# Moving six pieces of work between slots and engine queues in the first layer of a two-layer cross-attention and feed-forward kernel

## The chip, the cores and the metric

One NeuronCore of a Trainium2 chip runs the whole kernel. The metric is the device time of one execution in microseconds (us); lower is better. The engines are TensorE (PE; its weight loads are listed as PEld), VectorE (DVE), ScalarE (ACT), GpSimd (POOL) and SyncE (SP), which only issues DMAs here. Each engine runs its own instruction queue in order; semaphores join them.

## The reference, cut to what matters

```python
# x: (32, 256, 256), ctx: (32, 77, 192); 16 heads of 64
x = x + xattn0(layernorm(x), ctx, Wq0, Wk0, Wv0, Wo0, bo0)
x = x + ffn0(layernorm(x), w_gate, w_up, w_down)      # hidden 768, weights are integers / 127
x = x + xattn1(layernorm(x), ctx, Wq1, Wk1, Wv1, Wo1, bo1)
x = x + ffn1(layernorm(x), rhs)                       # rows and rhs rounded to 8-bit steps, product, rescaled

def xattn(x, c, Wq, Wk, Wv, Wo, bo):
    q, k, v = heads(x @ Wq), heads(c @ Wk), heads(c @ Wv)
    return softmax(q @ k.T / 8, axis=-1) @ v @ Wo + bo
def ffn0(x, w_gate, w_up, w_down):
    h = silu(x @ wg.T) * (x @ wu.T)
    return h @ wd.T
def layernorm(x): return (x - mean(x)) / sqrt(var(x) + 1e-5)
```

## The kernel before, in words

A first part (to about 230 us) prepares the weights and makes the keys and values of all 32 batches. The second part is a software pipeline over 64 bodies, one for each batch of layer 0 and then of layer 1, plus two to drain; the first layer's bodies are numbered h = 0 to 31. A body has four slots, u = 0 to 3, one for each unit of four heads. Float32 operands are split into a float16 "high" part (a cast on ACT, `high`, L348) and a "low" remainder (a subtraction on DVE, `low`, L362), so products come in two or three terms.

In slot u of body h each engine takes these steps, in an order that is written out by hand:

- PE: `scores` of unit u (L1237), `queries` two units ahead, the output product `project` four units back, `weigh_values` three units back (L1274), and pieces of the feed-forward of older batches: `gate_up(c)` is the product of hidden block c (six of them, gate and up), `down` the product back. `gate_up(0)` and `gate_up(1)` of batch h-2 are in slot 3, 2 to 5 in the next body's slots 0 and 1, both `down` in slot 2. Their input x2T comes by a DMA transposition of x216, the split second normalised rows.
- ACT: casts of attention output (oT_h) and queries (qT_h), `exponentials(k, i, t)` in two halves t (L1426, four heads each), `tanh_gate(c)` (L1406), casts of hidden blocks (hT_h), and `normalise` (L352), which applies scale and shift to rows: x_pair (xn) from x_in for the layer's next input, yn from y.
- DVE: row maxima nmax (L1549), reciprocals rden (L1554), low parts, `sigmoid_gate` (sg, L1514) and `hidden` (hf, L1525), row spreads (L378), their `moments` (L384, then ve at L386), `normalise_rows` (x2, L373), `out_rows` (y, L1536), and x1 (L1692) at the end of slot 3.
- POOL: `probabilities` in two halves (pr L1712, cast L1725, low part L1717), low parts of four hidden blocks (hT_l, L1703), and for each of the three normalisations `inverse` (rs, a power, L395); for the first and third also `shift` (nmr, L399 and L402).
- SP: all loads, stores and DMA transpositions in one queue, in the order of the code: pT (probabilities, two for each unit), x2T (`turn_second_rows`, slot 2), xT (`turn_rows`), keys, values, rows.

The next input batch b = h+2 of layer 0 goes through: spreads and moments (DVE, slot 2), inverse and shift (POOL, slot 2), `normalise` to xn (ACT, last thing in slot 2), `cast_rows` (ACT, x16 high), `low_rows` (DVE, x16 low), `turn_rows` (SP: in slot 3 for the first three bodies, in slot 0 of the next body from body 4 on). x16 is read by `turn_rows` only. The two lines below show how the queues are tied around the first two of these steps:

```python
pool.wait_ge(s_var[k], count)   # inverse: waits for ve of moments
act.wait_ge(s_nmr[0], h + 2)    # before normalise(act, xn, x_in, rs1, 0, s_xn)
```

Of the kernel before, what the change touches and what calls it, by code (L numbers as in the profile page):

```python
# [51 lines left out]
def xattn_ffn_kernel(nc, x, ctx, wq0, wk0, wv0, wo0, bo0, w_gate, w_up, w_down,  # L52
# [29 lines left out]
    with stack:  # L82
# [33 lines left out]
        mv1 = sb("mv1", [P, QT, 2], F32)  # L116
        ve1 = sb("ve1", [P, QT], F32)
# [881 lines left out]
        def as_f16(bank):  # L999

            return bank[:, 0, :].bitcast(F16).rearrange("p (k q) -> p k q", q=NQ)
# [101 lines left out]
        with nc.Block() as block:  # L1103
# [117 lines left out]
            def _(pe):  # L1221
# [100 lines left out]
                def body(h, like, lay, plan, odd):  # L1322
# [9 lines left out]
                    for u in range(UNITS):  # L1332
# [7 lines left out]
                        if u == 3 and lay[-2] == 0:  # L1340
                            pe.wait_ge(s_x2d, 16 * (h - 1))
                            if like == 2:
                                pe.wait_ge(s_kvf, RING + LATE_BASE + LATE - 1)
                            gate_up(0, bank("gu", 0))
# [19 lines left out]
                        if u == 3 and lay[-2] == 0:  # L1364
                            if like == 2:
                                pe.wait_ge(s_kvf, RING + LATE_BASE + LATE)
                            gate_up(1, bank("gu", 1))
# [9 lines left out]
                        if u == 2 and lay[-2] == 1:  # L1377
                            pe.wait_ge(s_qi, h - 1 - B)
                            turn(pe, as_f16(bank("turned_q", 0)), q_i).then_inc(s_qt, 1)
                        if three is not None and (like, u) != (NB, 2):  # L1380
                            weigh_values(n + u - 3, (u - 3) % UNITS, 16 * (h + (u - 3) // UNITS + 1),
                                         32 * (h + (u - 3) // UNITS + 1), OV)
# [11 lines left out]
            def _(act):  # L1394
                def body(h, like, lay, plan, odd):
# [34 lines left out]
                    for u in range(UNITS):  # L1430
# [4 lines left out]
                        if u == 3 and lay[2] == 0:  # L1435
                            cast_rows(act, h + 2)
# [47 lines left out]
                        if u == 3 and lay[-2] == 0:  # L1484
                            tanh_gate(0, h - 2)
                        if u == 3 and lay[-3] == 0:
                            act.wait_ge(s_nmr[2], h - 2)
                            act.wait_ge(s_ys, 16 * (h - 2))
                            normalise(act, yn, y, rs3, 2, s_yn)
                        if u == 3 and lay[-2] == 0:  # L1490
                            tanh_gate(1, h - 2)
                        if lay[0] is not None:
                            exponentials(n + u, u % 2, 1)
# [11 lines left out]
            def _(dve):  # L1505
                def body(h, like, lay, plan, odd):
# [49 lines left out]
                    for u in range(UNITS):  # L1556
                        if u == 3 and lay[-3] == 0:
                            moments(dve, 2, st3, mv3, ve3, s_st3, s_mv3, h - 3)
                        if u == 3 and lay[2] == 0:
                            low_rows(dve, h + 2)  # L1560
# [24 lines left out]
                        if u == 2 and lay[-2] == 0:  # L1585
                            dve.wait_ge(s_x216h, h - 1)
                            low(dve, x216[:, :, 1, :], x2[:, :, :], x216[:, :, 0, :]).then_inc(s_x216l, 1)
# [11 lines left out]
                        if u == 2 and lay[2] == 0:  # L1599
                            moments(dve, 0, st1, mv1, ve1, s_st, s_mv, h + 2)  # L1600
                        if u == 2 and lay[0] is not None and lay[-2] == 0:
                            reciprocals(n + u, u % 2, 0)
# [80 lines left out]
                        if u == 3 and lay[-1] is not None:  # L1683
# [6 lines left out]
                            if lay[-2] == 1:  # L1690
                                dve.wait_ge(s_ysum, h - 1 - B)
                            dve.scalar_tensor_tensor(out=x1[odd][:, :, :], in0=OA, scalar=O_DOWN, in1=x_res[:, :, :],  # L1692
                                                     op0=ALU.mult, op1=ALU.add).then_inc(s_x1, 1)

# [4 lines left out]
            def _(pool):  # L1699
                def body(h, like, lay, plan, odd):  # L1700
# [27 lines left out]
                    for u in range(UNITS):  # L1728
                        if u == 0 and lay[-3] == 0:
                            low_hidden(0, h - 3)  # L1730
                        if u == 1 and lay[-3] == 0:
                            low_hidden(3, h - 3)
                        if (like, u) == (NB - 1, 3):
# [13 lines left out]
                        if u == 2 and lay[2] == 0:  # L1747
                            inverse(pool, 0, ve1, rs1, h + 2)
                            shift(pool, 0, mv1, rs1, h + 2)
# [40 lines left out]
```

## Time and profile before

| | |
|---|---|
| median of three runs | 1650.83 us (1649.32 to 1656.25) |
| profiled execution, its own time | 1644.11 us |
| span from the first to the last instruction | 1642.1 us |
| granted TensorE clock, mean | 0.995 |
| busy over the span: PE, PEld | 93%, 81% |
| busy over the span: DVE, ACT, POOL | 85%, 80%, 75% |

The busy shares are means over three unlike stages: the preparation, the first layer (about 270 to 1060 us) and the second layer (from about 1090 us). A matmul counts as busy for longer than it holds the array back, since matmuls overlap. What a change in the first layer is worth is to be read from that stage alone: from the distance between the same instruction in two neighbouring bodies, and from who waits for whom inside a body.

### The profile page before, as it was taken

Reading aid. Unit: us, or ns where it says so; the run is one execution under the profiler, and the core shown is the slowest. Engines: PE = TensorE matmul, PEld = TensorE weight load, DVE = VectorE, ACT = ScalarE, POOL = GpSimd, SP = SyncE. Lnnn points to the kernel's source line nnn. Section 1 sums busy time; section 2 is a strip of 40 time slices with the busy share of each in tenths; the row PEclk is TensorE's granted clock in tenths of the full one; section 3 lists DMA queues with packets and bytes.
Section 4 is the critical chain, followed back from the end, with each engine's and each line's share of the span. In section 5 each row is a group of like instructions: output and inputs, shape, how many; then the busy total and the mean of one; then the engine's idle time right before and its main releaser. Section 6 shows DMA issues by size and latency. Waiting matters only on the chain.

```text
span 1642.1 us, 75141 instructions
## 1 busy us (share of the span) xinstructions
PE 1523.7 (93%) x27410; PEld 1326.2 (81%) x27410; DVE 1402.9 (85%) x3522; ACT 1311.8 (80%) x5514; POOL 1239.0 (75%) x1966
## 2 busy tenths in 40 slices
PE   7999888999999999999999999999999999999995
PEld 4555568888888888888888888988888888888884
DVE  7777558988888898888988887899999999999996
ACT  6656678887878778788887877788888888888883
POOL 5110277778888788878878887879999999999984
PEclk9999999999999999999999999999999999999998
DMA  8998699877787777777777898889889898898995
GB/s 267 349 307 278 190 182 188 151 173 159 161 169 167 175 159 165 170 159 171 163 175 154 164 170 160 165 161 198 197 193 195 197 195 191 195 201 191 189 186 118
DMA packets 740023, 307.79 MB, mean 187 GB/s; under 512 B 629201, under 2 KB 725361, under 8 KB 737841
## 3 DMA queue, kind: packets, MB, share of 16 engines
q1 hardware_dynamic: 738049, 299.32, 83.2%
q0 software_dynamic: 1840, 6.82, 1.4%
q8 instruction: 68, 1.11, 0.3%
q14 instruction: 66, 0.54, 0.1%
HBM read 87.09 MB, written 65.54 MB: 93 GB/s over the span
## 4 chain that ended last, share of the span: by engine, by line
PE 26%; POOL 19%; DVE 15%; issue 15%; ACT 8%; DMA 3%; SPq 2%; DVEq 1%; ACTq 0%; POOLq 0%
PE psum L333 17%; POOL pr L1712 7%; POOL p L1725 5%; POOL p L1717 5%; PE psum L1237 4%; PE psum L1274 4%; ACT ex L1426 4%; DVE nmax L1549 3%; DVE x L373 2%; DVE oT_l L362 2%; DMA x2T<-x 2%; ACT yn L352 1%; POOL rs L395 1%; DVE sg L1514 1%; DMA pT<-p 1%
## 5 line engine op out<-in xcount | busy, mean ns | idle before, releaser
L1426 ACT ACTIVATE ex<-psum,nmax 128x77 f32<-128x77 f32 x2048 | 636.1, 335 | 40.5 <-DVE nmax L1549 31.1
L1712 POOL TENSOR_TENSOR pr<-ex,rden 128x308 f32<-128x308 f32 x512 | 385.9, 754 | 81.7 <-DVE rden L1554 77.7
L1426 ACT ACTIVATION_READ_ACCUMULATOR ex<-psum,nmax 128x1 f32 x2048 | 443.4, 217 | 0.0
L1717 POOL TENSOR_TENSOR p<-pr,p 128x308 f16<-128x308 f32 x512 | 388.9, 760 | 40.7
L333 PE MATMUL psum<-xT,wq_h 128*64 128x256 f16 x4064 | 353.9, 276 | 0.8 <-DMA xT<-x 0.8
L1549 DVE TENSOR_REDUCE nmax<-psum 128x4 f32<-128x308 f32 x512 | 237.4, 464 | 57.4 <-PE psum L1237 57.2
L333 PE MATMUL psum<-xT,wq_l 128*64 128x256 f16 x2032 | 280.9, 273 | 0.0
L333 PE MATMUL psum<-wo_h,oT_h 128*64 128x256 f16 x1792 | 250.5, 276 | 27.7 <-DVE oT_l L362 27.4
L1725 POOL CAST p<-pr 128x308 f16<-128x308 f32 x509 | 238.8, 469 | 38.4 <-DMA pT<-p 5.8
L333 PE MATMUL psum<-wo_l,oT_h 128*64 128x256 f16 x1792 | 249.0, 274 | 0.0
L333 PE MATMUL psum<-wo_h,oT_l 128*64 128x256 f16 x1792 | 248.9, 274 | 0.0
L333 PEld LDWEIGHTS psum<-xT,wq_h 128*64 128x64 f16 x4064 | 208.4, 110 | 14.9 <-DMA xT<-x 0.9
L1274 PE MATMUL psum<-pT,vb 77*64 77x256 f16 x3072 | 212.8, 274 | 5.3 <-DMA pT<-p 5.3
L348 ACT ACTIVATE oT_h<-psum 128x512 f16<-128x512 f32 x256 | 153.5, 600 | 69.3 <-PE psum L1274 64.2
L1237 PEld LDWEIGHTS psum<-kb,qT_h 64*128 64x128 f16 x4096 | 115.1, 94 | 96.0 <-issue 96.0
L1237 PE MATMUL psum<-kb,qT_h 64*128 64x77 f16 x4096 | 145.1, 197 | 38.5 <-ACT ex L1426 19.7
L1274 PEld LDWEIGHTS psum<-pT,vb 77*64 77x64 f16 x3072 | 164.6, 110 | 15.6 <-issue 12.5
L362 DVE TENSOR_TENSOR oT_l<-psum,oT_h 128x512 f16<-128x512 f32 x256 | 174.2, 680 | 2.3 <-ACT oT_h L348 2.2
L365 DVE SCALAR_TENSOR_TENSOR qT_l<-psum,qT_h 128x512 f16<-128x512 f32 x256 | 173.1, 676 | 0.0
L348 ACT ACTIVATE qT_h<-psum 128x512 f16<-128x512 f32 x256 | 153.1, 598 | 3.5 <-PEq L412 3.5
L333 PEld LDWEIGHTS psum<-wo_h,oT_h 128*64 128x64 f16 x1792 | 102.3, 110 | 45.9 <-DVE oT_l L362 40.8
L1237 PE MATMUL psum<-kb,qT_l 64*128 64x77 f16 x2048 | 134.7, 194 | 0.0
(173 smaller groups left out, 3425.6 us busy)
## 6 DMA issues: line engine op xcount, KB each, us to landing
keys<-ks SPq DMA_DIRECT2D x16, 1232.0 KB, 7.4
kb<-keys SPq DMA_DIRECT2D x256, 77.0 KB, 2.7
vb<-vals SPq DMA_DIRECT2D x128, 154.0 KB
vals<-vs SPq DMA_DIRECT2D x64, 256.0 KB, 4.3
x_pair<-in_x_dram SPq DMA_DIRECT2D x32, 256.0 KB
pT<-p SPq DMA_TRANSPOSE x512, 3.3
x_res<-in_x_dram SPq DMA_DIRECT2D x32, 256.0 KB, 3.1
mid_x<-y SPq DMA_DIRECT2D x32, 256.0 KB, 2.5
```

The source lines that it names most:

```text
L333: last = pe.matmul(o[b * DH:(b + 1) * DH], w[:, b * DH:(b + 1) * DH], x, **flags)
L348: return act.activation(dst, src, ACT.Copy, scale=scale)
L362: return dve.tensor_tensor(dst, src, hi, ALU.subtract)
L365: return dve.scalar_tensor_tensor(out=qT_l[i][:, :, :], in0=src, scalar=Q_DOWN, in1=qT_h[i][:, :, :], op0=ALU.mult, op1=ALU.subtract)
L373: dve.tensor_scalar(dst[:, t, :], src[:, t, :], mv[:, t, 0:1], rs[:, t:t + 1], ALU.subtract, ALU.mult).then_inc(s_done, 1)
L1237: last = pe.matmul(SC[:, b, at], w[rows, a, t * P:(t + 1) * P], kb[u // 2][rows, b, part, u % 2 * PPU + a, :], start=(q == 0), stop=(q == ...
L1274: last = pe.matmul(o[b * DH:(b + 1) * DH, a, :].rearrange("p (t q) -> p t q", q=P), vb[u // 2][:, part, c:c + DH], pT[u][0:NK, b, at:at + ...
L1426: last = act.activation(ex[i][:, t, b, :], SC[:, t, b * NK:(b + 1) * NK], ACT.Exp, bias=nmax[i][:, t, b:b + 1], accum_out=den[i][:, t, b:b ...
L1549: dve.tensor_reduce(nmax[i][:, t, :], SC[:, t, :].rearrange("p (h k) -> p h k", k=NK), AX_X, ALU.max, negate=True).then_inc(s_m, 1)
L1712: pool.tensor_tensor(pr[:, t, :, :], ex[i][:, t, :, :], r, ALU.mult).then_inc(s_p, 1)
L1717: pool.tensor_tensor(d[:, t, 1, :, 0:NK], pr[:, t, :, :], d[:, t, 0, :, 0:NK], ALU.subtract).then_inc(s_pl, 1)
L1725: pool.tensor_copy(p16[v % 2][:, t, 0, :, 0:NK], pr[:, t, :, :]).then_inc(s_ph, 1)
```

## The change

Six moves, all in bodies that handle layer 0; no instruction is added, removed or resized.

1. PE, slot 3: `gate_up(0)` goes from behind `scores` to behind `queries`; `gate_up(1)` from behind `queries` to behind `project`.
2. ACT, slot 3: `cast_rows` goes from the head of the slot to behind `tanh_gate(0)`.
3. ACT, slot 3: `tanh_gate(1)` goes from ahead of the second half of the exponentials to behind it.
4. DVE, slot 3: `low_rows` goes from the head of the slot to its very end, behind x1.
5. DVE, slot 2: the low part of x216 goes from ahead of the spreads and moments of the next rows to behind them.
6. POOL, slot 2: `inverse` and `shift` of the next rows go from behind `probabilities(u-1, half 1)` to ahead of it.

```diff
--- before.py
+++ after.py
@@ -1337,11 +1337,6 @@
                             gate_up(4, bank("gu", 4))
                         if lay[0] is not None:
                             scores(n + u, u, 32 * (h + 1))
-                        if u == 3 and lay[-2] == 0:
-                            pe.wait_ge(s_x2d, 16 * (h - 1))
-                            if like == 2:
-                                pe.wait_ge(s_kvf, RING + LATE_BASE + LATE - 1)
-                            gate_up(0, bank("gu", 0))
                         if ("q", u) in plan:
                             if u == 2 and lay[1] == 0:
                                 pe.wait_ge(s_xd, 16 * (h + 1))
@@ -1362,9 +1357,10 @@
                             pe.wait_ge(s_nl, 16 * (h + 2 - B))
                             turn(pe, bank("turned_x", 0), xn).then_inc(s_xt, 1)
                         if u == 3 and lay[-2] == 0:
+                            pe.wait_ge(s_x2d, 16 * (h - 1))
                             if like == 2:
-                                pe.wait_ge(s_kvf, RING + LATE_BASE + LATE)
-                            gate_up(1, bank("gu", 1))
+                                pe.wait_ge(s_kvf, RING + LATE_BASE + LATE - 1)
+                            gate_up(0, bank("gu", 0))
                         if (like, u) == (NB, 2):
                             weigh_values(n + u - 3, (u - 3) % UNITS, 16 * (h + (u - 3) // UNITS + 1),
                                          32 * (h + (u - 3) // UNITS + 1), OV_END)
@@ -1377,6 +1373,10 @@
                         if u == 2 and lay[-2] == 1:
                             pe.wait_ge(s_qi, h - 1 - B)
                             turn(pe, as_f16(bank("turned_q", 0)), q_i).then_inc(s_qt, 1)
+                        if u == 3 and lay[-2] == 0:
+                            if like == 2:
+                                pe.wait_ge(s_kvf, RING + LATE_BASE + LATE)
+                            gate_up(1, bank("gu", 1))
                         if three is not None and (like, u) != (NB, 2):
                             weigh_values(n + u - 3, (u - 3) % UNITS, 16 * (h + (u - 3) // UNITS + 1),
                                          32 * (h + (u - 3) // UNITS + 1), OV)
@@ -1432,8 +1432,6 @@
                             high_hidden(0, h - 3)
                         if u == 1 and lay[-3] == 0:
                             high_hidden(2, h - 3)
-                        if u == 3 and lay[2] == 0:
-                            cast_rows(act, h + 2)
                         if lay[-1] is not None:
                             act.wait_ge(s_pv, n + u - 3)
                             high(act, oT_h[u % 2][:, :, :], weighed(like, u)).then_inc(s_oh, 1)
@@ -1483,14 +1481,16 @@
                                  bank("turned_x", 0).rearrange("p k (t q) -> p t k q", q=P)).then_inc(s_xh, 1)
                         if u == 3 and lay[-2] == 0:
                             tanh_gate(0, h - 2)
+                        if u == 3 and lay[2] == 0:
+                            cast_rows(act, h + 2)
                         if u == 3 and lay[-3] == 0:
                             act.wait_ge(s_nmr[2], h - 2)
                             act.wait_ge(s_ys, 16 * (h - 2))
                             normalise(act, yn, y, rs3, 2, s_yn)
+                        if lay[0] is not None:
+                            exponentials(n + u, u % 2, 1)
                         if u == 3 and lay[-2] == 0:
                             tanh_gate(1, h - 2)
-                        if lay[0] is not None:
-                            exponentials(n + u, u % 2, 1)
                         if u == 2 and lay[2] == 0:
                             act.wait_ge(s_nmr[0], h + 2)
                             act.wait_ge(s_x16l, h + 1)
@@ -1556,8 +1556,6 @@
                     for u in range(UNITS):
                         if u == 3 and lay[-3] == 0:
                             moments(dve, 2, st3, mv3, ve3, s_st3, s_mv3, h - 3)
-                        if u == 3 and lay[2] == 0:
-                            low_rows(dve, h + 2)
                         if lay[(u - 1) // UNITS] is not None:
                             reciprocals(n + u - 1, (u - 1) % 2, 1)
                         if lay[0] is not None:
@@ -1582,9 +1580,6 @@
                         if u == 1 and lay[-3] == 0:
                             sigmoid_gate(4, h - 3)
                             hidden(4, h - 3)
-                        if u == 2 and lay[-2] == 0:
-                            dve.wait_ge(s_x216h, h - 1)
-                            low(dve, x216[:, :, 1, :], x2[:, :, :], x216[:, :, 0, :]).then_inc(s_x216l, 1)
                         if u == 1 and lay[-2] == 1 and like <= NB:
                             normalise_rows(dve, 1, x2, x1[1 - odd], mv2, rs2, h - 1, s_x2)
                         if late_tile(like, u) is not None:
@@ -1598,6 +1593,9 @@
                             spreads(dve, x_in, st1, s_st)
                         if u == 2 and lay[2] == 0:
                             moments(dve, 0, st1, mv1, ve1, s_st, s_mv, h + 2)
+                        if u == 2 and lay[-2] == 0:
+                            dve.wait_ge(s_x216h, h - 1)
+                            low(dve, x216[:, :, 1, :], x2[:, :, :], x216[:, :, 0, :]).then_inc(s_x216l, 1)
                         if u == 2 and lay[0] is not None and lay[-2] == 0:
                             reciprocals(n + u, u % 2, 0)
                         if lay[(u + 1) // UNITS] is not None:
@@ -1691,6 +1689,8 @@
                                 dve.wait_ge(s_ysum, h - 1 - B)
                             dve.scalar_tensor_tensor(out=x1[odd][:, :, :], in0=OA, scalar=O_DOWN, in1=x_res[:, :, :],
                                                      op0=ALU.mult, op1=ALU.add).then_inc(s_x1, 1)
+                        if u == 3 and lay[2] == 0:
+                            low_rows(dve, h + 2)
 
                 bodies(dve, body)
 
@@ -1730,6 +1730,9 @@
                             low_hidden(0, h - 3)
                         if u == 1 and lay[-3] == 0:
                             low_hidden(3, h - 3)
+                        if u == 2 and lay[2] == 0:
+                            inverse(pool, 0, ve1, rs1, h + 2)
+                            shift(pool, 0, mv1, rs1, h + 2)
                         if (like, u) == (NB - 1, 3):
                             weights_of(h, 2, 1)
                         elif (like, u) == (NB, 0):
@@ -1744,9 +1747,6 @@
                             low_hidden(2, h - 3)
                         if u == 0 and (lay[-2] == 0 or lay[-3] == 0):
                             inverse(pool, 1, ve2, rs2, h - 1)
-                        if u == 2 and lay[2] == 0:
-                            inverse(pool, 0, ve1, rs1, h + 2)
-                            shift(pool, 0, mv1, rs1, h + 2)
                         if (like, u) == (NB - 1, 3):
                             weights_of(h, 3, 0)
                             low_of(h, 2, 1)
```

## Rows read from the trace of the kernel before

**Rows 1.** Waits over the span: us in total, times, longest.
```profile
ACT x_pair L352 <- POOL nmr L402: 88.8, 30, 3.1
```

**Rows 2.** Chain that ended last, 685 to 740 us: start, us, what.
```profile
719.15 0.20 POOL nmr L402
...
726.75 0.63 PE psum L1237 x24
```

**Rows 3.** Timeline, DVE's normalise_rows, one a body: start, us, instruction.
```profile
292.94 1.76 DVE L373 TENSOR_SCALAR x<-x,mv,rs 128x256 f32<-128x256 f32 x2
...
734.58 1.77 DVE L373 TENSOR_SCALAR x<-x,mv,rs 128x256 f32<-128x256 f32 x2
760.82 1.26 DVE L373 TENSOR_SCALAR x<-x,mv,rs 128x256 f32<-128x256 f32 x2
...
891.05 1.77 DVE L373 TENSOR_SCALAR x<-x,mv,rs 128x256 f32<-128x256 f32 x2
```

**Rows 4.** Timeline of DVE in one body, slots 2 and 3.
```profile
714.20 0.83 DVE L362 TENSOR_TENSOR x<-x 128x512 f16<-128x512 f32 x1
...
716.13 0.72 DVE L386 TENSOR_SCALAR ve<-mv 128x2 f32<-128x2 f32 x1
...
719.47 0.56 DVE L386 TENSOR_SCALAR ve<-mv 128x2 f32<-128x2 f32 x1
721.33 0.71 DVE L362 TENSOR_TENSOR x<-x_pair,x 128x512 f16<-128x512 f32 x1 [1.30 <-ACT x L348]
...
725.41 0.42 DVE L1514 SCALAR_TENSOR_TENSOR sg<-th,psum 128x256 f32<-128x256 f32 x1 [0.37 <-ACT th L1406]
...
727.37 0.48 DVE L1549 TENSOR_REDUCE nmax<-psum 128x4 f32<-128x308 f32 x1 [0.24 <-PE psum L1237]
```

**Rows 5.** Timeline of POOL in the same body.
```profile
714.54 0.79 POOL L1725 CAST p<-pr 128x308 f16<-128x308 f32 x1
...
716.12 0.70 POOL L1712 TENSOR_TENSOR pr<-ex,rden 128x308 f32<-128x308 f32 x1
716.89 0.44 POOL L1725 CAST p<-pr 128x308 f16<-128x308 f32 x1
...
718.12 0.69 POOL L395 TENSOR_TENSOR rs<-ve,half_neg 128x2 f32<-128x2 f32 x1
...
719.30 0.70 POOL L1712 TENSOR_TENSOR pr<-ex,rden 128x308 f32<-128x308 f32 x1
...
721.30 0.72 POOL L395 TENSOR_TENSOR rs<-ve,half_neg 128x2 f32<-128x2 f32 x1
...
726.55 0.70 POOL L1712 TENSOR_TENSOR pr<-ex,rden 128x308 f32<-128x308 f32 x1 [1.99 <-DVE rden L1554]
...
731.70 0.67 POOL L1703 TENSOR_TENSOR hT_l<-hf,hT_h 128x256 f16<-128x256 f32 x1 [0.42 <-ACT hT_h L348]
```

**Rows 6.** Timeline of ACT in the same body, slot 3.
```profile
724.00 1.11 ACT L352 ACTIVATE yn<-y,nmr,rs 128x256 f32<-128x256 f32 x2
724.99 0.40 ACT L1406 ACTIVATE th<-psum 128x256 f32<-128x256 f32 x1
```

**Rows 7.** A pair two hundred us on: DVE's low_rows, then POOL's power.
```profile
929.60 0.72 DVE L362 TENSOR_TENSOR x<-x_pair,x 128x512 f16<-128x512 f32 x1 [1.14 <-ACT x L348]
...
929.73 1.17 POOL L395 TENSOR_TENSOR rs<-ve,half_neg 128x2 f32<-128x2 f32 x1
```

**Rows 8.** SP and PE around x2T, and its landing time over the span.
```profile
715.54 1.26 SPq L1133 DMA_TRANSPOSE x2T<-x  x1
...
719.05 0.63 PE L333 MATMUL psum<-x2T,wgT 128*64 128x256 f16 x8
...
721.26 0.60 PE L333 MATMUL psum<-x2T,wgT 128*64 128x256 f16 x8
...
1006.58 0.63 PE L333 MATMUL psum<-x2T,wgT 128*64 128x256 f16 x8 [0.74 <-DMA x2T<-x]
...
DMA to landing us min/median/max: 3.3/3.4/5.2
```

## The prediction

> **What bounds the kernel now.** I read the waits over the whole span first. The largest one with an end to it on the first layer is ACT's: it stands about 3 us in each of 30 bodies before it can normalise the next rows, because POOL's shift comes late [rows 1]. A wait of an engine is worth nothing until it is on the chain, so the chain was read next, over two bodies around 712 us. It runs through POOL's probabilities to the shift at 719.15, then ACT's normalise and cast, DVE's low_rows, the exponentials of unit 3 and the scores of the next body at 726.75 [rows 2]. So the wait is on the path. The third view is one instruction that comes once a body. From 292.94 to 891.05 there are 24 of them, 23 periods, 26.00 us each [rows 3]; the period after a 1.77 us one is 26.24 us. 13 of the 24 take 1.77, the others 1.26; the short ones save 0.51 of the period. Last, the timelines of one body: DVE there idles only 1.30 us before low_rows, 0.37 before the second sg, 0.24 before the first maximum of the next body [rows 4]. That is 1.9 us in 26.24. DVE is the second bound, close behind the chain: of the 3 us that ACT waits, no more than about 1.9 can come back, and only if these three idles all vanish.
>
> **The moves, one by one**, in the times of the body of rows 4 to 6. No instruction is added, so each term is a start that moves.
>
> *DVE slot 2, POOL slot 2.* The x216 low part (0.83; the next instruction follows 0.75 later) leaves the place ahead of the spreads, so ve of the next rows comes to issue at 716.13 - 0.75 = 715.38 [rows 4]. POOL's cast beside that low part took 0.79 where the next cast took 0.44; without it POOL is free 0.35 earlier, at 716.12 - 0.35 = 715.8 [rows 5]. Power and shift can start at 715.9 instead of 718.12. But the low part now stands in DVE's queue straight behind ve, and the power waits for that same ve. What that does is seen at 929.6: low_rows began 0.13 before the power, and the power took 1.17 instead of 0.72 [rows 5, 7]. I take this 0.45, since the order of issue in the new code is the order of that pair; the lower bound is 0, from the power at 718.12. Then rs ends at 717.1 and nmr at 717.1 + (719.35 - 718.81) = 717.6, where 719.35 is the end of the shift and 718.81 that of the power [rows 2, 5]. ACT's normalise starts 1.7 us earlier. POOL's probabilities of the held half start at 717.1 + 0.5 = 717.6 instead of 716.12, last 2.0 (716.12 to 718.12), and the next half, at 719.30 before, starts at 719.6; its successor, the third norm's power, goes from 721.30 to 721.6. So nmr for yn is there at about 722.8 instead of 722.6.
>
> The Trainium skill (SBUF — State Buffer, section "Who interferes with whom") says that a DVE instruction with two SBUF inputs and a GpSimd instruction that reads SBUF hold the shared pair as an exclusive lock, and that the order of issue decides who blocks. The pair at 929.6 agrees (1.17 against 0.72). By that rule the low part behind ve stops the power for its whole length, and by the row for 0.45; either way the sum below stays within its bounds.
>
> *x2T.* The low part ends about 1.7 us later (about 716.75), so SP issues x2T at 716.8 instead of 715.54, and at 3.4 us to landing it is there at 720.2 [rows 8]. gate_up(0), at 719.05 before, stands behind the queries now. gate_up(0) and the queries, 40 matmuls, took 719.05 to 721.26, so the 24 of the queries take 1.33 and it comes at 720.4. The delay is covered by some 0.2 us. If the cover is gone, tanh_gate(0) comes late; it has about 0.4 until yn. SP's two pT issues behind x2T slip by 1.3 too; their reader, weigh_values in slot 0 of the next body, is far behind. I cost this at 0.
>
> *DVE slot 3, the head.* low_rows is gone, and with it the wait of 1.30. ve of the third norm cannot start sooner than about 719.4, since the second half of y waits for PE's second down product, and PE is dense. It ends, with POOL's instruction of that time, near 719.7, and the first maximum follows at 719.8; before it followed low_rows (721.33) by 0.7, at 722.0. It comes 2.2 us earlier, and the exponentials of unit 3, behind its 0.5, at 720.3.
>
> *ACT slot 3.* One half of the exponentials takes 1.2 (from the tanh at 724.99 to the scores at 726.75, less 0.3 for the tanh's step and 0.25 for the hand-over). So: exponentials 1.2, tanh_gate(0) 0.3, cast_rows 0.5 (0.63 less the overlap): ACT is free at 722.3, and yn waits for nmr until 722.8 (before: 724.00 [rows 6]). yn takes 1.0 (724.00 to 724.99), the second half of the exponentials 1.2, so tanh_gate(1), now behind them, starts at 725.0. It started at 724.99. Everything that was won ahead of it is spent: the exponentials end 1.4 us sooner, the tanh does not move.
>
> *DVE slot 3, the tail.* sg, hf, a reciprocal and x1 follow that tanh as before: sg at 725.45 against 725.41. Then comes low_rows. sg to the first maximum took 727.37 - 0.24 - 725.41 = 1.72 without its wait, 0.15 of it a last reciprocal, so low_rows issues 1.6 after sg, at 727.0, while POOL's pr of unit 3, which starts 0.24 after the reciprocal (726.55 before), holds on till 727.25 [rows 5]; low_rows without a hold needs 0.55 (0.83 less the 0.28 that pr covered at 714.20). It is done at 727.8, and the first maximum of the next body comes at 727.8 instead of 727.37: **+0.43 us**. Before, this maximum waited for the scores; they are now ready 1.3 us ahead, which is worth nothing. DVE is dense from there to slot 3, so the delay is passed on.
>
> *Given back.* PE's gate_up(3) is ready earlier, so ACT's tanh and the cast of hidden block 2 come 0.2 sooner against DVE, and POOL's low part of it, which waited 0.42 for that cast [rows 5], too. DVE's ve of the second norm ends with this POOL instruction, as ve at 716.13 ended with pr (716.85 and 716.82). **-0.2 us**; bounds 0 and -0.45, about the hold of rows 7.
>
> **The sum.** 0.43 - 0.2 = +0.23 us in each of the 27 bodies that have every step (h = 3 to 29): +6. In the four bodies behind them (from 976 us) there are no next rows, x2T lands late and PE stands 0.74 for it [rows 8]; the queries now fill that: 4 x -0.74 = -3. In the first three bodies turn_rows stands on SP in slot 3 behind low_rows, 5 us later than before, with the loads of x_res and keys queued behind it; these are needed late in the next body: 0 to +1, I take 0. Total +3 on the profiled 1644.1 us. The median of the runs shown is 6.7 us above that execution (1650.83 to 1644.11), so 1650.8 + 3 = **1654 us**.
>
> **The rivals.** I call "no change" what lies within 0.5% (8.3 us), about what a measurement of this kernel can tell.
>
> *Faster: the power is not held.* If it gets the port ahead of the low part (or reads its few values at once), nmr for yn is there at 722.35, ACT is the limit, and all of slot 3 shifts by 0.45: 27 x (0.23 - 0.45) - 3 = -9, about 1642. It gains another 0.24 a body (-6, 1636) if normalise_rows always takes 1.26: a mean 0.51 x 13/24 is lost now. For it: the power at 721.30 took only 0.72 with low_rows starting 0.03 behind it [rows 4, 5]. Against: there the power was first. Chance 0.27.
>
> *Slower: the tail is not given back.* If ve of the second norm stays held by POOL, for POOL's prob chain is itself held by low_rows (its cast waits until 727.8) and the low part of block 2 starts no earlier, the +0.43 stands, and up to 0.55 with a full collision: 27 x 0.5 - 3 = +10, 1661. It decides at the POOL instruction that runs when ve issues near 731.8. Chance 0.22.
>
> *Slower: POOL wins at normalise_rows.* It takes 1.77 or 1.26, in one body or the next, with nothing else changed [rows 3]: I read this as a race for the port with POOL's next instruction. If the new phase loses it in all bodies, 27 x 0.51 x 11/24 = +6 on top: 1660. Chance 0.09.
>
> *Nothing moves the end*, as worked out: 0.42, its own range 1648 to 1659.
>
> **Numbers.** 1654 is the likeliest case. The range 1638 to 1668 reaches from well into the first rival to both slower ones together. Faster by over 0.5% 0.27, within 0.42, slower 0.31.
>
> **What would show it.** In the trace after, in a steady body: the wait of ACT for nmr of the next rows falls from 3.1 to about 1.2; the power of the next rows takes about 1.17 and stands ahead of the first probabilities of slot 2; DVE waits some 2 us before its second sg (0.37 before) and none before the first maximum; low_rows takes about 0.8; the period, from normalise_rows, is 26.0 to 26.5. If the wait before sg is under 1 us, or the period is under 25.7, tanh_gate(1) comes earlier than I say and the prediction is wrong on the fast side. If PE waits for x2T, the cover was too thin and it is wrong on the slow side.

## The result and the profile after

The changed kernel takes 1657.26 us, the median of 20 runs (1653.88 to 1666.07), against 1649.16 us for the kernel before, also 20 runs on the same chips (1644.9 to 1656.25). The ratio is 1.0049 [1.0036, 1.0063]: slower by 0.5%, by more than the scatter of the runs and just inside what I called no change (8.1 us of 8.3). Forecast were 1654 us and a range of 1638 to 1668.

The profiled execution spans 1655.9 us against 1642.1. Of these 13.8 us, 5.4 lie ahead of the first normalise_rows of all (246.94 against 241.59). In the preparation of the weights POOL's one wait for DVE's moments (ve L608 <- mv L803) is 62.3 against 56.4, and the change doesn't touch that part. I put the 5.4 down to the execution: the twelve kernels below, which hold the same edits or parts of them, have 55.6 to 59.1 there. The times of the two profiled executions fit this: the one before is some 5 below its median, the one after 0.8 above. The rest, 8.4, is about that of the medians (8.1), and is told here.

Waits of the kernel after over the span (us, times, longest), beside [rows 1]:

```profile
ACT ex L1426 <- DVE nmax L1549: 93.9, 120, 1.6
DVE sg L1514 <- ACT th L1406: 85.9, 53, 2.8
...
ACT x_pair L352 <- POOL nmr L402: 38.8, 30, 1.6
```

The same view of the kernel before has these two:

```profile
ACT ex L1426 <- DVE nmax L1549: 31.1, 96, 1.1
...
DVE sg L1514 <- ACT th L1406: 12.2, 31, 1.1
```

ACT's wait for the mean product of the next rows fell from 88.8 to 38.8, what the change sets out to do. But DVE now waits 74 us longer for the tanh, and ACT 63 longer for the maxima. Fifty microseconds of waiting went, and more came back elsewhere.

DVE in one steady body, slots 2 and 3, and the normalise_rows on both sides (answers to [rows 3, 4]):

```profile
718.36 1.77 DVE L373 TENSOR_SCALAR x<-x,mv,rs 128x256 f32<-128x256 f32 x2
...
725.40 0.47 DVE L386 TENSOR_SCALAR ve<-mv 128x2 f32<-128x2 f32 x1
725.78 0.68 DVE L362 TENSOR_TENSOR x<-x 128x512 f16<-128x512 f32 x1
...
729.66 0.45 DVE L1549 TENSOR_REDUCE nmax<-psum 128x4 f32<-128x308 f32 x1
...
735.44 0.42 DVE L1514 SCALAR_TENSOR_TENSOR sg<-th,psum 128x256 f32<-128x256 f32 x1 [2.72 <-ACT th L1406]
...
736.99 0.83 DVE L362 TENSOR_TENSOR x<-x_pair,x 128x512 f16<-128x512 f32 x1
...
737.83 0.44 DVE L1549 TENSOR_REDUCE nmax<-psum 128x4 f32<-128x308 f32 x1
...
744.82 1.26 DVE L373 TENSOR_SCALAR x<-x,mv,rs 128x256 f32<-128x256 f32 x2
```

POOL in that body (answers to [rows 5]):

```profile
725.95 1.06 POOL L395 TENSOR_TENSOR rs<-ve,half_neg 128x2 f32<-128x2 f32 x1
...
727.36 0.20 POOL L402 TENSOR_TENSOR nmr<-nmr,rs 128x2 f32<-128x2 f32 x1
...
736.58 0.70 POOL L1712 TENSOR_TENSOR pr<-ex,rden 128x308 f32<-128x308 f32 x1 [1.79 <-DVE rden L1554]
...
741.93 0.67 POOL L1703 TENSOR_TENSOR hT_l<-hf,hT_h 128x256 f16<-128x256 f32 x1 [0.26 <-ACT hT_h L348]
```

ACT in slots 2 and 3 (answers to [rows 6]):

```profile
727.67 1.09 ACT L352 ACTIVATE x_pair<-x_pair,nmr,rs 128x256 f32<-128x256 f32 x2 [1.28 <-POOL nmr L402]
...
732.82 1.09 ACT L352 ACTIVATE yn<-y,nmr,rs 128x256 f32<-128x256 f32 x2 [0.49 <-POOL nmr L402]
...
735.02 0.38 ACT L1406 ACTIVATE th<-psum 128x256 f32<-128x256 f32 x1
```

Three distances divide the body. From normalise_rows to the second tanh: 735.02 - 718.36 = 16.66, and before 26.24 - (734.58 - 724.99) = 16.65. From that tanh to the first maximum of the next body: 737.83 - 735.02 = 2.81 against 727.37 - 724.99 = 2.38, so +0.43. From there to normalise_rows: 744.82 - 737.83 = 6.99 against 734.58 - 727.37 = 7.21, so -0.22 [rows 3, 4, 6]. The rows came earlier, the tanh did not, and low_rows behind it costs what it costs.

Normalise_rows over the first layer:

```profile
298.74 1.76 DVE L373 TENSOR_SCALAR x<-x,mv,rs 128x256 f32<-128x256 f32 x2
...
902.09 1.77 DVE L373 TENSOR_SCALAR x<-x,mv,rs 128x256 f32<-128x256 f32 x2
...
1005.42 1.67 DVE L373 TENSOR_SCALAR x<-x,mv,rs 128x256 f32<-128x256 f32 x2
...
1023.81 0.42 DVE L1514 SCALAR_TENSOR_TENSOR sg<-th,psum 128x256 f32<-128x256 f32 x1 [1.60 <-ACT th L1406]
...
1032.44 1.67 DVE L373 TENSOR_SCALAR x<-x,mv,rs 128x256 f32<-128x256 f32 x2
...
1109.24 1.65 DVE L373 TENSOR_SCALAR x<-x,mv,rs 128x256 f32<-128x256 f32 x2
```

and of the kernel before, the lines of the last bodies that its rows ahead do not have:

```profile
993.82 1.07 DVE L373 TENSOR_SCALAR x<-x,mv,rs 128x256 f32<-128x256 f32 x2
...
1010.38 0.42 DVE L1514 SCALAR_TENSOR_TENSOR sg<-th,psum 128x256 f32<-128x256 f32 x1 [0.36 <-ACT th L1406]
...
1013.23 0.48 DVE L1549 TENSOR_REDUCE nmax<-psum 128x4 f32<-128x308 f32 x1 [1.23 <-PE psum L1237]
...
1020.29 1.07 DVE L373 TENSOR_SCALAR x<-x,mv,rs 128x256 f32<-128x256 f32 x2
...
1095.13 1.64 DVE L373 TENSOR_SCALAR x<-x,mv,rs 128x256 f32<-128x256 f32 x2
```

The 23 steady periods take 603.35 / 23 = 26.23 us against 26.00 [rows 3]: +5.2 in all. The eight periods from there into the second layer take 207.15 (902.09 to 1109.24) against 204.08 (891.05 to 1095.13): +3.1. Together 8.3 of the 8.4; the first bodies add 0.45 (298.74 - 246.94 against 292.94 - 241.59), where I had taken 0 out of 0 to +1, and the second layer takes 0.3 less. In the last bodies of the layer (27.02 against 26.47 in the one shown) the second sg waits 1.60 for the tanh, 0.36 before, and normalise_rows takes 1.67, 1.07 before.

### The profile page after: what moved, and what is told of

Its sections match the earlier page's. It is cut to its first block, busy times and chain, and to the rows that moved or that the text cites. A ratio compares the mean times of both kernels' runs of the same rounds, so it can differ in the third digit from the quotient of the medians.

```text
span 1655.9 us, 75141 instructions
## 1 busy us (share of the span) xinstructions
PE 1528.6 (92%) x27410; PEld 1328.2 (80%) x27410; DVE 1380.2 (83%) x3522; ACT 1303.2 (79%) x5514; POOL 1251.2 (76%) x1966
## 4 chain that ended last, share of the span: by engine, by line
POOL 32%; DVE 24%; issue 21%; PE 5%; ACT 3%; DMA 1%; DVEq 1%; POOLq 0%; ACTq 0%; SPq 0%
POOL pr L1712 14%; POOL p L1725 8%; POOL p L1717 5%; PE psum L333 3%; DVE oT_l L362 3%; DVE nmax L1549 3%; POOL rs L395 3%; DVE sg L1514 3%; DVE x L373 3%; DVE st L378 3%; ACT ex L1426 2%; DVE qT_l L365 2%; DVE hT_l L362 1%; DVE hf L1525 1%; DVE ve L386 1%
## 5 line engine op out<-in xcount | busy, mean ns | idle before, releaser
L1426 ACT ACTIVATION_READ_ACCUMULATOR ex<-psum,nmax 128x1 f32 x2048 | 436.6, 213 | 0.0
L1514 DVE SCALAR_TENSOR_TENSOR sg<-th,psum 128x256 f32<-128x256 f32 x192 | 79.1, 412 | 87.2 <-ACT th L1406 85.9
```

Source lines behind the costliest of these rows:

```text
L1426: last = act.activation(ex[i][:, t, b, :], SC[:, t, b * NK:(b + 1) * NK], ACT.Exp, bias=nmax[i][:, t, b:b + 1], accum_out=den[i][:, t, b:b ...
L1514: dve.scalar_tensor_tensor(out=sg[:, c % 2, :], in0=th[:, c % 2, :], scalar=1.0, in1=bank("gu", c)[:, 0, :], op0=ALU.add, op1=ALU.mult).th ...
```

## The experiments

All ratios are to the kernel before on the same chip. "Period" is the distance from a normalise_rows of 1.26 us to the next one; after one of 1.77 us it is some 0.5 longer in every kernel, so the table compares like with like. The median of the kernel before was 1642.09 us beside e1 to e4, 1645.20 beside e5, e6, e8 and e9, 1649.28 beside e7, e10 and e11, and 1646.77 beside e12: medians of the table compare by their ratios.

| kernel | median us | ratio | period |
|---|---|---|---|
| before | 1649.16 | 1 | 25.74 |
| after | 1657.26 | 1.0049 [1.0036, 1.0063] | 25.96 |
| e1_tanh_ahead | 1616.78 | 0.9844 [0.9819, 0.9869] | 24.71 |
| e2_low_rows_gap | 1635.05 | 0.9950 [0.9933, 0.9967] | 25.30 |
| e3_power_first | 1654.30 | 1.0062 [1.0044, 1.0081] | 25.98 |
| e4_gates_back | 1650.89 | 1.0051 [1.0031, 1.0070] | 25.95 |
| e5_power_free | 1655.30 | 1.0055 [1.0036, 1.0073] | 25.94 |
| e6_tanh_behind | 1671.34 | 1.0159 [1.0137, 1.0182] | 26.53 |
| e7_tanh_and_gap | 1616.44 | 0.9799 [0.9782, 0.9816] | 24.50 |
| e8_deviation_ahead | 1630.13 | 0.9908 [0.9885, 0.9931] | 24.85 |
| e9_casts_late | 1630.13 | 0.9916 [0.9893, 0.9939] | 25.34 |
| e10, without tanh and products | 1628.85 | 0.9866 [0.9850, 0.9883] | 24.75 |
| e11_tanh_before_yn | 1632.08 | 0.9899 [0.9883, 0.9916] | 24.75 |
| e12_low_between_rows | 1634.20 | 0.9914 [0.9891, 0.9936] | 24.80 |

**The changed kernel with the tanh ahead again.**

```diff
+                        if u == 3 and lay[-2] == 0:
+                            tanh_gate(1, h - 2)
                         if lay[0] is not None:
                             exponentials(n + u, u % 2, 1)
-                        if u == 3 and lay[-2] == 0:
-                            tanh_gate(1, h - 2)
```

> The changed kernel with tanh_gate(1) put back ahead of the second half of the exponentials on ACT; nothing else differs from it. Theory of the prediction: the first maximum of the next body hangs on that tanh (DVE waits 2.72 us for it at 735.44), so the tanh comes 1.2 us sooner, the scores become the next limit, and the period of a steady body falls from 26.22 by about 1.0 to 1.2, to 25.0 to 25.3: some 25 to 30 us off the changed kernel, ratio to the kernel before 0.985 to 0.992. Rival (DVE is the bound whatever ACT does, or PE is): the period falls by under 0.3 and the ratio stays at 1.00 to 1.005.

Two blocks swapped turn 0.5% slower into 1.6% faster, 1.25 us a body, a little more than the 1.0 to 1.2 expected. Normalise_rows and the second sg in its timeline:

```profile
732.75 0.42 DVE L1514 SCALAR_TENSOR_TENSOR sg<-th,psum 128x256 f32<-128x256 f32 x1 [1.49 <-ACT th L1406]
...
742.12 1.26 DVE L373 TENSOR_SCALAR x<-x,mv,rs 128x256 f32<-128x256 f32 x2
...
766.83 1.26 DVE L373 TENSOR_SCALAR x<-x,mv,rs 128x256 f32<-128x256 f32 x2
```

The wait fell from 2.72 to 1.49, by 1.23, and the period by 1.25: the wait for the tanh was on the path with its full length.

**The kernel before with only that move**, tanh_gate(1) behind the exponentials (the same two blocks swapped the other way).

> The kernel before with one edit: the second tanh of the gates stands behind the second four exponentials of the fourth slot, as in the changed kernel; all the rest as before. Theory (the gated product on VectorE waits last for this tanh in every body): its wait of some 2 us grows by the 1.2 us of the exponentials, less what they gain, 0.8 to 1.2 a body over 31 bodies: 25 to 37 us, ratio 1.015 to 1.023. Rival (the place of the tanh matters only together with the moved casts): ratio 1.000 to 1.004.

```profile
720.45 1.26 DVE L373 TENSOR_SCALAR x<-x,mv,rs 128x256 f32<-128x256 f32 x2
...
738.26 0.42 DVE L1514 SCALAR_TENSOR_TENSOR sg<-th,psum 128x256 f32<-128x256 f32 x1 [1.60 <-ACT th L1406]
...
747.00 1.26 DVE L373 TENSOR_SCALAR x<-x,mv,rs 128x256 f32<-128x256 f32 x2
```

Slower by 1.6%. The period of 26.53 (26.55 in the pair shown) is 0.8 above 25.74, the lower edge of what I gave. DVE's wait before sg grows by 1.23, to 1.60 (it was 0.37 [rows 4], and not the "some 2 us" of my expectation). Part comes back, as the exponentials that went ahead of the tanh feed the next waits: DVE's 0.24 for the scores [rows 4] is gone. The same edit costs 1.25 in the new order, where nothing gives it back.

**The two halves of the change, alone.** In the kernel before, first the deviation:

```diff
+                        if u == 2 and lay[2] == 0:
+                            inverse(pool, 0, ve1, rs1, h + 2)
+                            shift(pool, 0, mv1, rs1, h + 2)
                         if (like, u) == (NB - 1, 3):
                             weights_of(h, 2, 1)
...
-                        if u == 2 and lay[2] == 0:
-                            inverse(pool, 0, ve1, rs1, h + 2)
-                            shift(pool, 0, mv1, rs1, h + 2)
```

and on DVE the x216 low part behind the moments, as in the changed kernel.

> The kernel before with one part of the change: the power and the mean's product of the next rows stand ahead of the probabilities on GpSimd in the third slot, and the low part of the second norm's rows stands behind the moments on VectorE. Casts, tanh and the products on TensorE as before. Theory (this part moves the third norm's rows by 0.2 later and frees only time that ScalarE waits for): -0.1 to +0.1 a body, ratio 0.998 to 1.002. Rival (the deviation is what the 26 us of the version with the tanh ahead come from, since normalise on ScalarE starts 1.7 us earlier): -0.6 to -0.8 a body, ratio 0.985 to 0.989.

```profile
722.36 1.26 DVE L373 TENSOR_SCALAR x<-x,mv,rs 128x256 f32<-128x256 f32 x2
...
747.22 1.25 DVE L373 TENSOR_SCALAR x<-x,mv,rs 128x256 f32<-128x256 f32 x2
```

Then cast_rows behind tanh_gate(0) on ACT and low_rows at the end of the slot on DVE, and nothing else.

> The kernel before with the other part alone: the cast of the next rows behind the first tanh on ScalarE and their low part at the end of the fourth slot on VectorE; deviation, tanh and the products on TensorE as before. Theory (the low part of 0.8 us stood ahead of the first maximum of the fourth slot, on the way to the exponentials and the third norm): 0.3 to 0.6 less in a body, ratio 0.989 to 0.995, and with the part of the deviation alone it adds up to about 0.985. Rival (neither part is worth anything alone, each one's gain is held by the other): ratio 0.998 to 1.002.

The first gives 0.9908, 0.89 us a body, and my theory for it was wrong: I had taken the time that comes earlier on ACT for free time. In its rows the 1.30 that DVE waited before low_rows [rows 4] are gone, and 0.40 before the second half of y and 0.4 more before the second sg have come in. The rival had the cause, with a period above its 0.6 to 0.8 and a ratio short of its 0.985 to 0.989. The gain of the periods doesn't reach the median in full: the 23 steady ones take 23.4 us less, the median is 15.1 less, and the profiled execution is 2.4 us longer up to its first normalise_rows, 1.9 in the first bodies and 2.5 in the second layer. Of these only the 1.9 lie where the edit acts. The second gives 0.9916, 0.40 a body, as expected. Each half is a gain of its own, and neither is held by the other.

**Both halves, without the tanh and without the products on TensorE.**

> The kernel before with the deviation ahead and the casts late, both parts together, tanh and the products on TensorE as before. Together with the version of the change that has only its tanh put back, it prices the moved products once more. Theory (the products' place is neutral): the period is that of the other version, 24.7 where the normalise takes 1.26, ratio 0.983 to 0.987. Rival (with the tanh ahead the second gate product must be early): 0.2 to 0.5 less, ratio 0.977 to 0.982.

0.9866: 1.0 us a body, less than 0.89 + 0.40 = 1.29, so 0.3 is won by both. **The products alone** were tried from the other side, the changed kernel with gate_up(0) and gate_up(1) where they stood before.

> The changed kernel with PE's order of the kernel before: gate_up(0) ahead of the queries, gate_up(1) behind them. Theory: x2T lands about 1.3 us later than in the kernel before, so PE waits about 0.9 us for it ahead of the queries, but PE has room in slot 3 and tanh_gate(0) is held by the exponentials; a steady body stays within 0.1 of 26.22 and the ratio is 1.003 to 1.008. Rival (the move on PE is what keeps the changed kernel from being slower still): period 26.5 or more, ratio 1.01 or more; if the move itself does harm, ratio under 1.002.

1.0051 against 1.0049, and a period of 25.95 against 25.96: the place of the products is worth nothing there. PE waits about 0.8 for x2T in every steady body of it, and in none of the changed kernel, so this wait is not on the path. With the tanh ahead, the moved products give 0.9844 and the old ones 0.9866; the intervals overlap.

**Low_rows where DVE waits.** In the changed kernel, between hidden(0) and sigmoid_gate(1):

```diff
                             hidden(0, h - 2)
+                        if u == 3 and lay[2] == 0:
+                            low_rows(dve, h + 2)
+                        if u == 3 and lay[-2] == 0:
                             sigmoid_gate(1, h - 2)
...
-                        if u == 3 and lay[2] == 0:
-                            low_rows(dve, h + 2)
```

> The changed kernel with low_rows taken from the end of slot 3 into the 2.72 us in which DVE waits for the second tanh (between hidden(0) and sigmoid_gate(1)). Theory: low_rows at the slot's end costs its whole step of 0.76 in each body, so the period falls by 0.7 to 0.8 (26.22 to about 25.5), 20 us, ratio 0.990 to 0.995. Rival (the first maximum would wait for the scores or something else anyway): under 0.2 a body, ratio 1.00 to 1.005.

0.66 less in a body, just under the 0.7 to 0.8 expected, and the ratio is at the edge of its range. One body at the layer's end took 28.6. **And with the tanh ahead as well:**

> The changed kernel with two edits: the second tanh back ahead of the second exponentials, and the low part of the next rows between the first gated product and the second one on VectorE, where it waited 1.49 for that tanh. Each edit alone gave a period of 24.71 and 25.30 (where the rows' normalise takes 1.26), against 25.96. Theory (both take from the same wait): the wait of 1.49 falls to 0.7, and the 0.83 at the end of the slot is gone: 24.1 to 24.5, ratio to the kernel before 0.975 to 0.982. Rival (TensorE or the exponentials end last once 24.7 is reached): 24.6 to 24.75, ratio 0.983 to 0.987.

The wait before sg is 0.89 and the period 24.50; the rival's 24.6 was passed, my 24.1 to 24.5 just reached. At 0.9799 this is the best version, 2.0% under the kernel before and 2.5% under the changed one.

**The hold of the power.** By a hold I mean that a POOL instruction takes longer because a DVE instruction with two inputs in SBUF is running. The prediction priced the low part that stands behind ve at 0.45 on the power. Three edits try to take it away. In the changed kernel, the low part behind the reciprocal:

> The changed kernel with the low part of x216 one place later on DVE, behind the reciprocal of 0.09 us, so that POOL's power is issued before it. Theory: the power then takes 0.69 to 0.72 instead of 1.06, nmr of yn comes 0.35 sooner, ACT no longer stands 0.49 for it, and the period falls by 0.3 to 0.4, 9 us, ratio 0.998 to 1.001. Rival (the power's length is not on the path, or the low part is stopped instead for as long): period within 0.1 of 26.22, ratio 1.003 to 1.007.

```profile
744.19 0.47 DVE L386 TENSOR_SCALAR ve<-mv 128x2 f32<-128x2 f32 x1
...
744.65 0.65 DVE L362 TENSOR_TENSOR x<-x 128x512 f16<-128x512 f32 x1
744.73 1.12 POOL L395 TENSOR_TENSOR rs<-ve,half_neg 128x2 f32<-128x2 f32 x1
```

A miss of the test, not of the theory: POOL begins so late after ve that the low part was still 0.08 ahead. So it was put behind the low part of the queries:

> The changed kernel with the low part of the second norm's rows (TENSOR_TENSOR x<-x) moved behind the low part of the queries in the third slot, so that some 0.75 us lie between the deviation of the next rows and the first operation with two operands of the SBUF. Theory (the hold costs, part of the +0.22 a body is the power stretched from 0.7 to 1.06): the power takes 0.68 to 0.75, the mean's product lands 0.35 earlier, yn waits 0.2 or less instead of 0.49, and a body loses 0.15 to 0.35: ratio to the kernel before 0.997 to 1.002, against 1.005 of the change. Rival (the hold is slack because tanh waits behind the exponentials anyway): the power is short but the period stays at 26.2, ratio 1.004 to 1.006. A third way: the rows turned for the gates (x2T) land 0.7 later and the first gate product waits for them, ratio 1.008 or more.

```profile
718.97 0.47 DVE L386 TENSOR_SCALAR ve<-mv 128x2 f32<-128x2 f32 x1
...
719.53 0.69 POOL L395 TENSOR_TENSOR rs<-ve,half_neg 128x2 f32<-128x2 f32 x1
720.02 0.67 DVE L362 TENSOR_TENSOR x<-x 128x512 f16<-128x512 f32 x1
720.19 0.60 POOL L399 TENSOR_SCALAR nmr<-mv 128x2 f32<-128x2 f32 x1
720.93 0.20 POOL L402 TENSOR_TENSOR nmr<-nmr,rs 128x2 f32<-128x2 f32 x1
```

The power is free (0.69), and the next of the three is held instead: 0.60 for an instruction that takes 0.23 elsewhere. From ve to the end of the three it is 721.13 - 718.97 = 2.16, in the changed kernel 727.56 - 725.40 = 2.16. The hold changed its place and kept its length, and the period stayed with it (25.94), as the rival had it; its reason stays untested. Last, in the best version, between the two sums of y:

> The version with the second tanh ahead and the low part of the next rows in the gap (period 24.50 where the normalise takes 1.26), and in it the low part of the second norm's rows between the two row sums of the output (y), where VectorE waited 0.39 for TensorE in every body. One place later than the low part of the queries had only moved the hold: the power took 0.69 instead of 1.06, but the mean's product behind it 0.60 instead of 0.23. Theory (the hold is on the path while the three short operations of GpSimd and the low part overlap): here the low part starts 1.1 later than now, the three are nearly through, ScalarE's rows start some 0.3 earlier, VectorE saves the wait of 0.39, and a body loses 0.2 to 0.4: period 24.1 to 24.3, ratio to the kernel before 0.970 to 0.977. Rival (the rows turned for the gate products are issued 1.1 later: they landed 0.48 ahead of their first product, so TensorE and the first tanh wait 0.6, and the transposes of the probabilities behind them on the queue go up to 1 later): 24.6 or more, ratio 0.982 or more.

```profile
732.58 0.47 DVE L386 TENSOR_SCALAR ve<-mv 128x2 f32<-128x2 f32 x1
733.12 0.69 POOL L395 TENSOR_TENSOR rs<-ve,half_neg 128x2 f32<-128x2 f32 x1
733.78 0.23 POOL L399 TENSOR_SCALAR nmr<-mv 128x2 f32<-128x2 f32 x1
733.95 0.67 DVE L362 TENSOR_TENSOR x<-x 128x512 f16<-128x512 f32 x1
734.16 0.52 POOL L402 TENSOR_TENSOR nmr<-nmr,rs 128x2 f32<-128x2 f32 x1
...
737.97 0.63 PE L333 MATMUL psum<-x2T,wgT 128*64 128x256 f16 x8 [0.37 <-DMA x2T<-x]
```

Now the third is held (0.52 for 0.20), and the rival came on top: x2T is issued late enough that PE waits for it, and the kernel loses 1.2% against the version it was made from. The steady bodies lose 0.3 each; two bodies at the layer's end took 28.5 and 30.8, and PE waited 2.13 for x2T in the second of them. What the hold costs is thus still open: none of the edits took it away.

**The tanh ahead of yn**, in e10: one step further up on ACT.

> As the kernel with deviation ahead and casts late, tanh and products as before, and in it the second tanh one step further ahead: before the normalise of yn, which waits for GpSimd's mean product, instead of behind it. Theory (VectorE's wait of 1.49 is for a tanh that stands behind yn and its wait of 0.49 for GpSimd): the tanh starts some 1.2 earlier, the wait falls to 0.3 to 0.6, 0.5 to 0.9 less in a body, period 23.8 to 24.2, ratio 0.969 to 0.978. Rival (yn then starts 0.1 to 0.3 later and its exponentials with it, so that the next wait, for the exponentials, takes it back): period 24.5 to 24.7, ratio 0.982 to 0.986.

ACT in its slot 3:

```profile
734.73 0.38 ACT L1406 ACTIVATE th<-psum 128x256 f32<-128x256 f32 x1 [0.84 <-PE psum L333]
735.01 1.08 ACT L352 ACTIVATE yn<-y,nmr,rs 128x256 f32<-128x256 f32 x2
```

DVE's wait fell (1.55 to 0.86), the time did not: 0.9899 against 0.9866. No gain was near the rival's outcome (24.5 to 24.7, ratio 0.982 to 0.986), but by another way than it gave. ACT's queue now stands 0.84 for the second gate product of TensorE, with yn and the exponentials behind it.

## Why the prediction was right, and where it was not

*ve, power and mean product.* I said that the power would be held by the low part behind ve and take 1.17 instead of 0.72; it took 1.06. The wait of ACT for the next rows' mean product is 1.28 in a steady body (1.2 forecast). The Trainium skill (SBUF — State Buffer, "Who interferes with whom") has the holder decided by the order of issue; the runs agree, with 1.12 for a power that issued 0.08 behind the low part and 0.69 for one issued 0.49 ahead of it. The extra in the body shown is 1.06 - 0.69 = 0.37, and 725.78 + 0.68 - 725.95 = 0.51 of the low part was left when the power began. I had taken 0.45 over from rows 7 as it stood, but the length follows what is left of the low part: it is that less 0.14 in all four kernels shown (last section).

*"Everything that was won ahead of it is spent."* The tanh stands 16.66 from normalise_rows, 16.65 before, as worked out. The experiments say who spends it. The deviation and the casts give 1.0 a body together, and the tanh behind the exponentials takes 1.25. One number hid two of opposite sign. I had said "some 2 us" for DVE's wait before the second sg; it is 2.72, and my own terms gave 0.37 + 2.2 = 2.6.

*The tail.* +0.43 for low_rows and -0.2 given back; measured +0.43 and -0.22. The giving back went the way I said, too: POOL waits 0.26 for the cast of block 2 where it waited 0.42, and ve of the second norm ends with POOL's instruction (742.63 and 742.60). The sum of +0.23 a body is +0.23 by the 23 steady periods. The rival "the tail is not given back" is out: it asked for +0.5. "POOL wins at normalise_rows" is out for the steady bodies, where 13 of the first 24 take 1.77, as before; at the end of the layer it is not, as told below.

*The rival "the power is not held"* is out as stated, the power was held. Its gain was not tested, for no run removed the hold. Its further gain from a short normalise_rows was put at 0.24 a body; 0.51 x 13/24 is 0.28.

*x2T and the products* cost nothing, as said: PE has no wait for x2T in the steady body, and the run with the old order is level.

**The step that failed: "4 x -0.74 = -3" for the last bodies of the layer.** From 902 us into the second layer the measured difference is +3.1; I had -3 there and some +0.9 of the steady bodies. The last four periods alone take 103.82 (1005.42 to 1109.24) against 101.31 (993.82 to 1095.13): +2.5 instead of -3, and the forecast of +3 in all should have been about +8. That the median still fell well inside my range is owed to the width of the range.

The sum had two faults there. First, PE's wait for x2T did go, but it was not on the path. The changed kernel with the tanh ahead has no such wait in its last four periods either, and they take 101.27 us:

```profile
967.35 1.06 DVE L373 TENSOR_SCALAR x<-x,mv,rs 128x256 f32<-128x256 f32 x2
...
1068.62 1.64 DVE L373 TENSOR_SCALAR x<-x,mv,rs 128x256 f32<-128x256 f32 x2
```

The kernel before takes 101.31 with waits of 0.74 and 0.66 for x2T in two of the four; the other two have none, so 4 was too many as well.

Second, the +2.5 come with the tanh behind the exponentials: the kernel before with that edit alone takes 104.03 there. But the longer wait for the tanh is not what is paid. In the body shown, normalise_rows to the second sg takes 18.39 against 16.56, of which 1.24 is the wait and 0.60 the normalise_rows itself; from there to the next normalise_rows it is 8.63 against 9.91, since DVE no longer waits 1.23 for the scores. The wait is given back, and +0.55 is left, about what normalise_rows takes longer. It does so in three of the four bodies (1.67 for 1.07 to 1.09), and by 0.20 in the fourth: some 2.0 of the 2.5. That the length is paid in full shows in the best version, which has both lengths in these bodies:

```profile
967.18 1.67 DVE L373 TENSOR_SCALAR x<-x,mv,rs 128x256 f32<-128x256 f32 x2
...
994.05 1.06 DVE L373 TENSOR_SCALAR x<-x,mv,rs 128x256 f32<-128x256 f32 x2
```

The first body takes 26.87 (967.18 to 994.05); the same body of the kernel with the tanh ahead, which has the same order there, since no low_rows of next rows is left, takes 26.25 with a normalise_rows of 1.06. So the rival "POOL wins at normalise_rows" had the right event, at the end of the layer instead of in the steady bodies. In the six kernels with the tanh behind, 17 of the 18 normalise_rows of these three bodies take 1.66 or 1.67; in the eight with it ahead, 2 of 24 do. So the place of the tanh sets how often it is long; by what collision is not shown.

## What to carry to other kernels

When several moves are judged as one and the sum is near zero, price each move from the state that the others leave: here one swap of two blocks hid a version that is 1.6% faster than the one before. An instruction put behind others on its engine "because nothing waits for it" is to be checked against who waits for its result next: here DVE, 1.2 us, in every body. A wait that a change removes is worth nothing until it is shown to be on the path: PE's 0.8 for x2T came and went in every body without a trace in the period. And a stage whose input is missing at the ends of a pipeline needs a sum of its own.

## What was not expected of the hardware

A low part of 128x512 with both inputs in SBUF (0.65 to 0.68 us) lengthened whichever small POOL instruction began while it ran: a power of 128x2 from 0.69 to 1.06 or 1.12, a tensor_scalar from 0.23 to 0.60, a tensor_tensor from 0.20 to 0.52. The extra is 0.32 to 0.43, and it follows one rule in the four kernels shown: what was left of the low part when the POOL instruction began, less 0.14.

| kernel | low part ends | POOL begins | left | extra |
|---|---|---|---|---|
| after | 726.46 | 725.95 | 0.51 | 0.37 |
| e3_power_first | 745.30 | 744.73 | 0.57 | 0.43 |
| e5_power_free | 720.69 | 720.19 | 0.50 | 0.37 |
| e12_low_between_rows | 734.62 | 734.16 | 0.46 | 0.32 |

In the traces of these four it is 0.13 to 0.16 in each of the 26 bodies with such a pair between 300 and 1060 us. So it is as if the small instruction had only 0.14 us of its time behind it when the low part is through, though it had begun 0.08 to 0.21 us into it. With all three POOL instructions in a row, moving the low part by 0.7 or 1.0 us against ve left the end of the three where it was, to within 0.06 us.
